# A decoder layer with experts on one core: expert rows fetched five tiles ahead, and a head's convolution products taken from cyclic copies that ScalarE writes

## The chip, the core and the metric

The kernel runs on one core of a Trainium2 chip. The metric is the device time of one execution in microseconds (us). Engines by their names in the profile: PE is TensorE (PEld its weight loads), DVE is VectorE, ACT is ScalarE, POOL is GpSimd, SP is SyncE; SP, ACT and POOL also start DMAs. On chip data lies in SBUF, 128 partitions wide, and PE writes to PSUM.

## What is computed

```python
x = x + attn(layernorm(x))                               # 16 heads, ALiBi, 16 x 256 tokens of 512
x = x + conv(k=ctx, v=ctx, q=layernorm(x), ssm_kernel, D)  # below
x = x + experts(layernorm(x))                            # top 2 of 8, silu-gated, 512 -> 256 -> 512

# conv: B=16, H=32 heads of 8 channels, length L=512
kv = einsum('bhil,bhjl->bijhl', k_, v_)                  # all 8 x 8 channel pairs of a head
y = irfft(rfft(kv, 2L) * rfft(ssm_kernel, 2L))[..., :L]  # causal convolution along L
out = einsum('bijhl,bhil->bjhl', y + kv * D, q_)
```

Since k and v are both the context, the pair (i, j) equals (j, i): 36 of the 64 pairs are distinct.

## The kernel before

The program has four stages, one after another: attention (up to about 720 us of the profiled execution), the convolution (743 to 1144), routing with the split of the expert weights (1156 to 1300), and the expert tiles (1300 to 1803).

**Convolution.** L lies across the partitions, in four chunks of 128 (EC). The batches are done in two groups g of 8 (GB), and in a group the 32 heads (SH) one after another: 64 steps in all, with h the head's number. Everything of a head has two buffers, by its parity. For one head and one group:
- POOL, `form_pairs` (L1037), multiplies the context by itself into `pairs`, 36 columns for each of 4 x 8 (chunk, batch): 8 TENSOR_TENSORs, one for each run of pairs that `pair_segments` gives, 1152 elements a partition. It waits for PE to be done with head h-2 (y_ready).
- PE, `convolve` (L1087), multiplies `pairs` by `taps` (a skewed view of the filter that SP loads): 10 products of 288 columns, which are 20 MATMUL records, into the PSUM tile `ps_y`. It waits for the pairs, the taps, and until DVE has read the `ps_y` of head h-2 (prods_ready).
- DVE, `multiply` (L1155), multiplies `ps_y` by q into `prods`, 15 TENSOR_TENSORs of 32 to 256 elements, 2048 in all. The eight terms of one sum lie side by side in `prods`, so each instruction writes its elements 8 apart (32 bytes).
- POOL, `fold` (L1046), adds the last two of the eight terms to the first two (512 elements).
- DVE, `add_up` (L1174), sums the remaining six (one TENSOR_REDUCE, 1536 elements) back over q.

DVE's order is multiply(h), add_up(h-1), multiply(h+1), add_up(h). POOL's is form_pairs(h), fold(h-2). ACT has nothing to do while the heads run.

**Experts.** The token rows are sorted by expert into 72 tiles of 128 (N_TILES). The loops are unrolled by RING tiles (8 before); rings of BUFS = 4 hold the fetched rows `srow` and the outputs `y_row`. For tile n:
- SP loads `pair_row` (which tokens), DVE `read_pairs` turns it into the indices `take` and `back`.
- POOL, `gather` (L1492), fetches 128 rows of 2 KB from DRAM into `srow` by an indirect DMA. POOL's step for tile n is: gather(n + AHEAD) with AHEAD = 3, wait for `y_row` of tile n, wait until the scatter of tile n-1 has landed, then the scatter of tile n, an indirect DMA that adds `y_row` to the output in DRAM (L1513). Tiles of one expert have no token in common, tiles of two experts may.
- PE's step for tile n is: transposes of the rows of tile n+2 (`s_transposes`, L1588), `h_transposes` of tile n (L1612), `gate_and_up` of tile n+1 (L1601, 12 matmuls), `down_rows` of tile n (L1621). So the rows of tile n+3 are needed at the start of step n+1.
- ACT and DVE move tiles from PSUM to SBUF between these steps; ACT's `weigh` (L1705) writes `y_row`.

## Time and profile before

| what | value |
|---|---|
| time, median of 3 runs | 1803.71 us (1803.37 to 1810.03) |
| the profiled execution | 1810.99 us, its span 1809.1 us |
| mean granted clock of PE | 0.929 of full |
| PE busy / DVE / ACT / POOL | 84% / 63% / 38% / 39% of the span |
| convolution, one head | 5.65 us, 64 heads |
| expert tiles | 72, from 1304 us to the end |

The span runs from the first to the last instruction; 1.9 us of the execution lie around it. Busy shares are averages over four stages that have different limits, so they are read by stage.

### The profile page before, as it was taken

The page shows a single profiled execution, that of the slowest core. Times are in us where ns is not written, and L with a number is a line of the kernel's source. Part 1 is how long each engine was busy: PE and PEld are TensorE (multiplying, and loading weights), DVE is VectorE, ACT ScalarE, POOL GpSimd, SP SyncE. Part 2 cuts the span into 40 slices and gives each one's busy share as a digit, 9 for nine tenths or more (in the row PEclk, how much of TensorE's full clock was granted, in tenths as well). Part 3 has the DMA queues.
Part 4 walks back from the last instruction along what each step waited for, and adds up shares of the span by engine and source line. Part 5 has one row for each costly group of instructions (what it writes and reads, how often), then busy time and mean ns, then how long its engine had stood idle before and what let it go on. Part 6 is the DMA issues. An engine that isn't in the chain of part 4 may idle for free. (4 is left out here: it accounts for less than half of the span.)

```text
span 1809.1 us, 34128 instructions
## 1 busy us (share of the span) xinstructions
PE 1513.5 (84%) x8665; PEld 1192.7 (66%) x8666; DVE 1141.0 (63%) x3591; ACT 678.5 (38%) x1818; POOL 712.3 (39%) x1160
## 2 busy tenths in 40 slices
PE   4999999999999997799968888667187888878886
PEld 4888888888888885666656666567155555555554
DVE  5788777777777776699989999866422222222221
ACT  3777677767676776100001000023122222222222
POOL 2111111111111101688846888266633343344343
PEclk9999999999999999999989999655599999899999
DMA  5543333433343445411131111369534444344441
GB/s 168 122 106 95 94 93 93 110 94 93 95 109 92 109 97 216 151 46 47 46 116 36 47 45 34 128 162 259 128 66 74 76 72 73 66 78 79 72 79 35
DMA packets 89767, 172.13 MB, mean 95 GB/s; under 512 B 26384, under 2 KB 26384, under 8 KB 88656
## 3 DMA queue, kind: packets, MB, share of 16 engines
q1 hardware_dynamic: 63584, 122.46, 25.3%
q0 software_dynamic: 18176, 35.80, 11.0%
q10 hardware_dynamic: 7920, 12.93, 2.8%
q8 instruction: 27, 0.44, 0.1%
q14 instruction: 60, 0.49, 0.1%
HBM read 78.10 MB, written 44.79 MB: 68 GB/s over the span
## 5 line engine op out<-in xcount | busy, mean ns | idle before, releaser
L1097 PE MATMUL ps_y<-pairs,taps 128*128 128x288 f32 x1280 | 324.5, 410 | 35.4 <-DVE prods L1170 32.1
L1097 PEld LDWEIGHTS ps_y<-pairs,taps 128*128 128x128 f32 x1280 | 238.3, 190 | 121.1 <-POOL pairs L1041 41.6
L853 ACT ACTIVATE probs<-neg_scores,neg_max 128x256 f32<-128x256 f32 x512 | 255.2, 505 | 26.1 <-DVE neg_max L654 25.9
L1170 DVE TENSOR_TENSOR prods<-ps_y,q_g 128x224 f32<-128x224 f32 (+7 forms) x960 | 251.3, 402 | 17.7 <-issue 8.0
L654 DVE CUSTOM_DVE_ANT_0 neg_scores<-ps_scores,alibi 128x256 f32<-128x256 f32 x512 | 194.8, 418 | 91.0 <-PE ps_scores L519 60.4
L1041 POOL TENSOR_TENSOR pairs<-ctx_g 128x32 f32 (+11 forms) x512 | 215.5, 460 | 43.0 <-PE ps_y L1097 31.8
L1513 POOL DMA_INDIRECT out<-y_row,back x72 | 113.2, 1573 | 293.1 <-ACT y_row L1705 158.3
L1894 DVE TENSOR_TENSOR st_lo<-ps_x,st_hi 128x512 fp32r<-128x512 f32 x72 | 49.8, 691 | 249.2 <-ACT st_hi L1690 249.2
L863 ACT ACTIVATE probs_t<-ps_probs_t 128x512 f32<-128x512 f32 x208 | 124.0, 596 | 130.5 <-PE ps_probs_t L530 130.4
L530 PE MATMUL ps_probs_t<-ident,probs 128*128 128x128 f32 x1024 | 159.2, 279 | 8.9 <-ACT probs L853 8.9
L1588 PE MATMUL ps_x<-ident,srow 128*128 128x128 f32 x288 | 49.1, 296 | 121.0 <-DMA srow<-xn_rows,take 120.8
L1588 PEld LDWEIGHTS ps_x<-ident,srow 128*128 128x128 f32 x288 | 32.5, 146 | 175.9 <-DMA srow<-xn_rows,take 95.8
L403 POOL COPY inv_wide<-inv_sum 128x512 f32<-128x512 f32 x32 | 20.6, 672 | 318.1 <-DVE inv_sum L670 318.1
L530 PEld LDWEIGHTS ps_probs_t<-ident,probs 128*128 128x128 f32 x1024 | 124.3, 143 | 22.7 <-ACT probs L853 9.4
L1621 PE MATMUL ps_down<-w_down,hidden_t 128*128 x288 | 135.3, 592 | 0.6 <-DVE hidden_t L1884 0.6
L519 PE MATMUL ps_scores<-k_stack,q_stack 96*128 96x256 f32 x512 | 128.5, 334 | 6.3 <-DMA k_stack<-k_lo 5.7
L1601 PE MATMUL ps_gu<-w_gu_hi,st_hi 128*128 x288 | 124.7, 433 | 0.3 <-DVE st_lo L1894 0.3
L1050 POOL TENSOR_TENSOR prods<-prods 128x512 f32<-128x512 f32 x64 | 98.6, 1541 | 64.9 <-DVE prods L1170 64.9
L1601 PE MATMUL ps_gu<-w_gu_hi,st_lo 128*128 x288 | 117.9, 409 | 0.0
L1601 PE MATMUL ps_gu<-w_gu_lo,st_hi 128*128 x288 | 117.6, 408 | 0.0
L1888 DVE TENSOR_TENSOR hidden<-ps_gu,silu_g 128x256 f32<-128x256 f32 x72 | 30.6, 424 | 131.4 <-ACT silu_g L1697 131.4
L1176 DVE TENSOR_REDUCE q_g<-prods 128x1536 f32 (+1 forms) x64 | 110.4, 1725 | 0.6 <-POOL prods L1050 0.6
(185 smaller groups left out, 3287.2 us busy)
## 6 DMA issues: line engine op xcount, KB each, us to landing
q_stack<-q_hi SPq DMA_DIRECT2D x128, 128.0 KB, 2.3
k_stack<-k_hi SPq DMA_DIRECT2D x128, 128.0 KB, 2.3
taps<-kernel_pad SPq DMA_DIRECT2D x64, 256.0 KB, 3.1
x_in<-in_x SPq DMA_DIRECT2D x16, 512.0 KB, 3.5
q_stack<-q_lo SPq DMA_DIRECT2D x64, 128.0 KB, 2.3
k_stack<-k_lo SPq DMA_DIRECT2D x64, 128.0 KB, 2.3
x_rows<-x_mid SPq DMA_DIRECT2D x16, 512.0 KB, 3.0
ctx_g<-in_ctx_t SPq DMA_DIRECT2D x2, 4096.0 KB, 12.4
```

The lines of the kernel that those rows point to most:

```text
L519: last = pe.matmul(ps_scores[h % 2][:, tt, :], q_stack[:, r, c, tt * P:tt * P + P], k_stack[:, r, c, :], start=True, stop=True)
L530: last = pe.transpose(ps_probs_t[h % 2][:, jt, tt * P:tt * P + P], probs[h % 2][:, tt, jt * P:jt * P + P], ident[:])
L654: last = dve.tensor_tensor_reduce(neg_scores[h % 2][:, tt, :], ps_scores[h % 2][:, tt, :], alibi[h % 2][:, P - P * tt:P - P * tt + T], -Q_ ...
L853: last = act.activation(probs[h % 2][:, tt, :], neg_scores[h % 2][:, tt, :], ACT.Exp, bias=neg_max[par][:, h, tt:tt + 1], scale=-1.0, accu ...
L863: act.activation(probs_t[h % (2 * HPC)][:], ps_probs_t[h % 2][:], ACT.Copy).then_inc(probs_t_kept[h % 2], 1)
L1041: last = pool.tensor_tensor(pairs[par][:, :, :, col:col + n], head_of(ctx_g, k * 2 + par, i, n), head_of(ctx_g, k * 2 + par, j, n), ALU.mult)
L1097: last = pe.matmul(ps_y[par][:, lc, 0:GB * PAIRS], taps[r][:, block_cols:block_cols + P], pairs[par][:, mc, :, :], start=(mc == 0), stop=( ...
L1170: last = dve.tensor_tensor(prods[par][:, :, :, to:to + n, term], y[:, :, :, col:col + n], head_of(q_g, own, q_from, n), ALU.mult)
L1176: dve.tensor_reduce(head_of(q_g, k * 2 + par, 0, SD), prods[par][:, :, :, :, 0:SD - FOLD], AX_X, ALU.add).then_inc(z_ready, 1)
L1513: pool.indirect_dma_start(out=out_rows, out_offset=bass.IndirectOffsetOnAxis(ap=back[r][:, 0:1], axis=0), in_=y_row[r % BUFS][:], in_offse ...
L1601: last = pe.matmul(ps_gu[:, r % 2, :], st[r % 2][x_part][:, c, :], w_gu[w_part][:, ds(e, 1), c, :].rearrange("p o f -> p (o f)"), start=(c ...
L1621: last = pe.matmul(ps_down[:, r % 2, :], hidden_t[r % 2][:, c, :], w_down[:, ds(e, 1), c, :].rearrange("p o f -> p (o f)"), start=(c == 0) ...
```

## The change

Two independent edits, one in the convolution and one in the expert stage.

**Convolution.** With d the cyclic distance of the two channels of a pair, `pairs` is now formed by two POOL instructions: all pairs with d = 0 to 3 at once (1024 elements), reading the context's 8 channels and a doubled copy of them, `ctx_ring`, at a moving start, and the four with d = 4 (128 elements). ACT writes `ctx_ring` (512 elements) and, for q, `q_ring` (512). When PE is done with a head, ACT copies `ps_y` into `y_rows`, with the first elements of each row repeated behind it: three ACTIVATEs of 1024, 288 and 256 elements. DVE then multiplies `y_rows` by `q_ring` in four instructions (one of 1280 elements, three of 256) that read and write consecutive elements, with the eight terms of a sum now 8 elements apart; one TENSOR_REDUCE of all 2048 reads them at that stride. `fold` is gone. PE waits for ACT's copy (y_kept) instead of DVE's products, DVE too.

**Experts.** RING 12, AHEAD 5, and six `srow` buffers (ROW_BUFS); `y_row` keeps four. The scatter of tile n waits for the landing of tile n-2, and for that of tile n-1 only where the expert changes. Which it is stands in a table, `tile_wait_i`, that DVE computes in three more instructions in routing, and POOL reads by a register load ahead of each scatter.

```diff
@@ convolution, POOL
-                    for col, i, j, n in pair_segments():
-                        last = pool.tensor_tensor(pairs[par][:, :, :, col:col + n],
-                                                  head_of(ctx_g, k * 2 + par, i, n),
-                                                  head_of(ctx_g, k * 2 + par, j, n), ALU.mult)
-                    last.then_inc(pairs_ready, 1)
-                def fold(g, k, par):
...
+                    wait_apart(pool, ctx_ring_ready, k * 2 + (g * SH + par + 1), passed)
+                    own = by_lane(ctx_g, k * 2 + par)
+                    to = pairs[par][:, :, :, :].rearrange("p m b q -> p (m b) q")
+                    pool.tensor_tensor(to[:, :, 0:HALF * SD].rearrange("p n (d i) -> p n d i", i=SD),
+                                       own.unsqueeze(2).to_broadcast([P, EC * GB, HALF, SD]),
+                                       turned(ctx_ring[par], HALF), ALU.mult)
+                    pool.tensor_tensor(to[:, :, HALF * SD:PAIRS], own[:, :, 0:HALF], own[:, :, HALF:SD], ALU.mult)\
+                        .then_inc(pairs_ready, 1)
@@ convolution, PE
-                    pe.wait_ge(prods_ready, h + (1 - 2 + PRODS_START))
+                    pe.wait_ge(y_kept, h + (1 - 2 + KEPT_START))
@@ convolution, ACT (head h: keep_y, then turn_ctx of head h + 2)
+                def turn_ctx(g, k, par):
...
+                        act.wait_ge(pairs_ready, k * 2 + (g * SH + par - 1))
...
+                    ring_of(ctx_ring[par], ctx_g, k * 2 + par).then_inc(ctx_ring_ready, 1)
+                def keep_y(g, k, par):
+                    act.wait_ge(prods_ready, h + (1 - 2 + PRODS_START))
+                    ring_of(q_ring[par], q_g, k * 2 + par)
+                    act.wait_ge(y_ready, h + (1 + Y_START))
...
+                    act.activation(whole_rows[:, :, :, 0:SD], near, ACT.Copy)
+                    act.activation(whole_rows[:, :, 0:HALF - 1, SD:ROW], near[:, :, 1:HALF, SD - HALF + 1:SD], ACT.Copy)
+                    act.activation(rows[:, :, HALF * ROW:ROWS].rearrange("p n (u i) -> p n u i", u=2),
...
+                                   ACT.Copy).then_inc(y_kept, 1)
@@ convolution, DVE
+                    dve.wait_ge(y_kept, h + (1 + KEPT_START))
                     dve.wait_ge(z_ready, h + (1 - 2 + Z_START))
...
+                    dve.tensor_tensor(prods[par][:, :, 0:HALF + 1, :], main_rows(y_rows[par], HALF + 1),
+                                      turned(q_ring[par], HALF + 1), ALU.mult)
+                    for e in range(HALF + 1, SD):
+                        d = SD - e
+                        last = dve.tensor_tensor(prods[par][:, :, e, :], y_rows[par][:, :, d * ROW - d:d * ROW - d + SD],
+                                                 q_ring[par][:, :, e:e + SD], ALU.mult)
...
+                    dve.tensor_reduce(by_lane(q_g, k * 2 + par), prods[par][:].rearrange("p n e i -> p n i e"), AX_X,
@@ experts, POOL
-        RING = 8
+        RING = 12
-        AHEAD = 3
+        ROW_BUFS = 6
+        AHEAD = 5
...
+                        landed = pool.value_load(tile_wait_i[0:1, ds(tile_no(kk, r) - 1, 1)], min_val=16,
+                                                 max_val=N_TILES // BUFS * 16)
                     wait_apart(pool, y_ready, tile_no(kk, r) + 1 + Y_START, passed)
-                        wait_apart(pool, y_scattered[(r - 1) % BUFS], turn(kk, r - 1) * 16 + 16, passed)
+                        wait_apart(pool, y_scattered[(r - 2) % BUFS], turn(kk, r - 2) * 16 + 16, passed)
...
+                        wait_apart(pool, y_scattered[(r - 1) % BUFS], landed, passed)
@@ routing, DVE
+                chain(dve.tensor_tensor(new_expert[:, 0:N_TILES - 1], tile_expert[:, 1:N_TILES],
+                                        tile_expert[:, 0:N_TILES - 1], ALU.not_equal))
+                dve.scalar_tensor_tensor(tile_wait_i[:, 0:N_TILES - 1], new_expert[:, 0:N_TILES - 1], 16.0,
+                                         turn_f[:, 0:N_TILES - 1], ALU.mult, ALU.add).then_inc(tiles_known, 1)
```

DVE's queue in the loop over heads, before, for one head (the sum between is that of the head before):

```order
L1170 TENSOR_TENSOR prods<-ps_y,q_g 128x256
L1170 ISA
L1170 TENSOR_TENSOR prods<-ps_y,q_g 128x32x7 x2
L1170 TENSOR_TENSOR prods<-ps_y,q_g 128x32
L1170 ISA
L1170 TENSOR_TENSOR prods<-ps_y,q_g 128x32
L1170 ISA
L1170 TENSOR_TENSOR prods<-ps_y,q_g 128x32x6 x2
```

The same place of DVE's queue now, the four products of one head and the sum of the head before:

```order
L1208 TENSOR_TENSOR prods<-y_rows,q_ring 128x32x40
L1212 TENSOR_TENSOR prods<-y_rows,q_ring 128x32x8 x3
L26 ISA
L1220 ISA
L1220 TENSOR_REDUCE q_g<-prods 128x32x8
```

Fifteen products that read PSUM and q have become four that read two SBUF tiles. ACT's queue at the same place, empty before, now holds for one head:

```order
L1135 ACTIVATE q_ring<-q_g 128x512
L1151 REGISTER_ALU
L1156 ACTIVATE y_rows<-ps_y 128x32x4x8
L1157 ACTIVATE y_rows<-ps_y 128x32x3x3
L1158 ACTIVATE y_rows<-ps_y 128x32x8
L1141 ISA
L1135 ISA
L1135 ACTIVATE ctx_ring<-ctx_g 128x512
```

The copy of the context for head h+2 stands behind the three copies of head h. POOL's queue at the start of the expert tiles, before:

```order
L1500 DMA srow<-xn_rows,take 128x512 x4
L1513 DMA out<-y_row,back 4096x512
L1500 DMA srow<-xn_rows,take 128x512
L1513 DMA out<-y_row,back 4096x512
L1500 DMA srow<-xn_rows,take 128x512
```

And now, from the start:

```order
L1555 DMA srow<-xn_rows,take 128x512 x6
L1577 DMA out<-y_row,back 4096x512
L1555 DMA srow<-xn_rows,take 128x512
L1577 DMA out<-y_row,back 4096x512
L1555 DMA srow<-xn_rows,take 128x512
```

Six fetches stand ahead of the first scatter instead of four. From the sixth tile on it reads:

```order
L1555 DMA srow<-xn_rows,take 128x512
L1565 TENSOR_LOAD tile_wait_i
L1565 ISA x2
L1577 DMA out<-y_row,back 4096x512
L1555 DMA srow<-xn_rows,take 128x512
```

A register load now stands between the fetch and the scatter.

## Rows read from the trace of the kernel before

**Rows 1.** Stretches: us; PE, PEld, DVE, ACT, POOL busy; clock; DMA share; GB/s
```profile
780.00:900.00 120.00, 108.18 (x427) 79.08 (x427) 116.89 (x337) 0.00 (x0) 102.98 (x191) 1.00 0.17 47
...
1324.00:1540.00 216.00, 173.86 (x702) 116.99 (x703) 49.83 (x160) 52.37 (x95) 83.08 (x64) 0.98 0.42 74
```
**Rows 2.** PE in order of time, heads: start, us, op, [idle before <-releaser]
```profile
808.03 5.09 PE L1097 MATMUL ps_y<-pairs,taps 128*128 128x288 f32 x20 [0.56 <-DVE prods L1170]
```
**Rows 3.** DVE in order of time, the same heads
```profile
803.95 3.93 DVE L1170 TENSOR_TENSOR prods<-ps_y,q_g 128x256 f32<-128x256 f32 x15
807.74 1.73 DVE L1176 TENSOR_REDUCE q_g<-prods 128x1536 f32 x1
```
**Rows 4.** Who waited for whom, 1300 to 1800 us: total, times, longest
```profile
PE ps_x L1588 <- DMA srow<-xn_rows,take: 120.8, 60, 26.1
```
**Rows 5.** The transposes of the fetched rows, L1588: ns min/median/max, first and last start
```profile
L1588 PE MATMUL ps_x<-ident,srow x288: 272/273/475, 1304.3 to 1787.9; 128*128 128x128 f32 x144
```
**Rows 6.** The chain that ended last, 1400 to 1440 us
```profile
1412.63 0.70 ACT y_row L1705
...
1414.32 0.02 POOL out L1513
...
1416.20 4.32 DMA srow<-xn_rows,take
```
**Rows 7.** PE in order of time around one tile whose rows had landed
```profile
1550.41 1.88 PE L1621 MATMUL ps_down<-w_down,hidden_t 128*128 x4
1552.13 0.60 PE L1588 MATMUL ps_x<-ident,srow 128*128 128x128 f32 x4
...
1555.55 1.88 PE L1621 MATMUL ps_down<-w_down,hidden_t 128*128 x4
1559.44 0.66 PE L1588 MATMUL ps_x<-ident,srow 128*128 128x128 f32 x4 [2.02 <-DMA srow<-xn_rows,take]
```
**Rows 8.** POOL in order of time, expert tiles
```profile
1537.95 1.58 POOL L1513 DMA_INDIRECT out<-y_row,back  x1 [6.20 <-issue]
1539.84 1.05 POOL L1500 DMA_INDIRECT srow<-xn_rows,take  x1 [0.30 <-issue]
1543.70 1.57 POOL L1513 DMA_INDIRECT out<-y_row,back  x1 [2.81 <-DMA out<-y_row,back]
```
**Rows 9.** Register loads of SP, L1442 (columns as in rows 5)
```profile
L1442 SPq TENSOR_LOAD <-tile_row_i x72: 263/268/480, 1296.7 to 1750.8; - x72
```
**Rows 10.** DVE, groups by form: busy, mean ns, idle before
```profile
L1170 DVE TENSOR_TENSOR prods<-ps_y,q_g 128x256 f32<-128x256 f32 x64 | 40.1, 626 | 17.7 <-issue 8.0 <-DVE q_g L1176 2.4 <-PE ps_y L1097 0.8
...
L1888 DVE TENSOR_TENSOR hidden<-ps_gu,silu_g 128x256 f32<-128x256 f32 x72 | 30.6, 424 | 131.4 <-ACT silu_g L1697 131.4
...
L1402 DVE TENSOR_TENSOR w_gu_lo<-w_half,w_gu_hi 128x1024 f32 x4 | 4.9, 1226 | 2.3 <-DVEq L1809 2.3
```
**Rows 11.** ACT, groups by form
```profile
L863 ACT ACTIVATE probs_t<-ps_probs_t 128x512 f32<-128x512 f32 x208 | 124.0, 596 | 130.5 <-PE ps_probs_t L530 130.4
...
L1132 ACT ACTIVATE q_g<-ps_y 128x1024 f32 x16 | 16.3, 1027 | 223.1 <-PE ps_y L1083 223.1
```
**Rows 12.** POOL, groups by form
```profile
L1402 POOL TENSOR_TENSOR w_gu_lo<-w_half,w_gu_hi 128x1024 fp32r<-128x1024 f32 x4 | 9.4, 2354 | 0.7 <-ACT w_gu_hi L1658 0.7
...
L1041 POOL TENSOR_TENSOR pairs<-ctx_g 128x128 f32 x60 | 27.4, 456 | 0.0
```
**Rows 13.** DVE in order of time, routing
```profile
1225.87 1.23 DVE L1402 TENSOR_TENSOR w_gu_lo<-w_half,w_gu_hi 128x1024 f32 x1 [0.55 <-DVEq L1809]
...
1256.85 0.19 DVE L1757 TENSOR_TENSOR is_best<-ps_gu,best 128x32 f32<-128x32 f32 x1
1257.18 0.63 DVE L1758 TENSOR_TENSOR is_best<-is_best,backward 128x32 f32<-128x32 f32 x1
```
**Rows 14.** POOL in order of time, routing
```profile
1226.45 2.85 POOL L1402 TENSOR_TENSOR w_gu_lo<-w_half,w_gu_hi 128x1024 f32 x1 [4.19 <-ACT w_gu_hi L1658]
...
1254.94 2.82 POOL L1402 TENSOR_TENSOR w_gu_lo<-w_half,w_gu_hi 128x1024 f32 x1 [1.15 <-ACT w_gu_hi L1658]
```

More of the change, by code:

```diff
@@ L961, in build_decoder @@
         TAP_BUFS = 4
-        FOLD = 2
-        def pair_segments():
-            segments = [(0, 0, 0, SD)]
-            for d in range(1, SD // 2):
-                segments += [(d * SD, 0, d, SD - d), (d * SD + SD - d, SD - d, 0, d)]
-            return segments + [(SD // 2 * SD, 0, SD // 2, SD // 2)]
+        HALF = SD // 2
+        ROW = SD + HALF - 1
+        ROWS = HALF * ROW + SD
         with ExitStack() as scope:
@@ L981, in build_decoder @@
             pairs = [sb(f"pairs{i}", [P, EC, GB, PAIRS]) for i in range(2)]
-            prods = [sb(f"prods{i}", [P, EC, GB, SD, SD]) for i in range(2)]
+            prods = [sb(f"prods{i}", [P, EC * GB, SD, SD]) for i in range(2)]
+            y_rows = [sb(f"y_rows{i}", [P, EC * GB, ROWS]) for i in range(2)]
+            q_ring = [sb(f"q_ring{i}", [P, EC * GB, 2 * SD]) for i in range(2)]
+            ctx_ring = [sb(f"ctx_ring{i}", [P, EC * GB, 2 * SD]) for i in range(2)]
             xn_g = [sb(f"xn_g{i}", [P, TT, E]) for i in range(2)]
@@ L1062, in _ @@
                             form_pairs(g, k, par)
-                            fold(g, k - 1, par)
-                    for par in range(2):
-                        fold(g, SH // 2 - 1, par)
                 pool.wait_ge(x2_moments, GT)
@@ L1096, in convolve @@
                             block_cols = (lc - mc) * P
-                            last = pe.matmul(ps_y[par][:, lc, 0:GB * PAIRS], taps[r][:, block_cols:block_cols + P],
+                            last = pe.matmul(ps_y[par][:, lc, :].rearrange("p (b q) -> p b q", b=GB)[:, :, 0:PAIRS],
+                                             taps[r][:, block_cols:block_cols + P],
                                              pairs[par][:, mc, :, :], start=(mc == 0), stop=(mc == lc))
@@ L1123, in _, with ring_of @@
                 act.sem_inc(c_xt_kept, XT_START)
+                act.sem_inc(y_kept, KEPT_START)
+                def ring_of(to, tile, h):
+                    return act.activation(to[:].rearrange("p n (u i) -> p n u i", u=2),
+                                          by_lane(tile, h).unsqueeze(2).to_broadcast([P, EC * GB, 2, SD]), ACT.Copy)
+                def turn_ctx(g, k, par):
+                    if not (isinstance(k, int) and k == 0):
+                        act.wait_ge(pairs_ready, k * 2 + (g * SH + par - 1))
+                    elif g:
+                        act.wait_ge(pairs_ready, SH)
+                    ring_of(ctx_ring[par], ctx_g, k * 2 + par).then_inc(ctx_ring_ready, 1)
+                def keep_y(g, k, par):
+                    h = k * 2 + (par + g * SH)
+                    act.wait_ge(prods_ready, h + (1 - 2 + PRODS_START))
+                    ring_of(q_ring[par], q_g, k * 2 + par)
+                    act.wait_ge(y_ready, h + (1 + Y_START))
+                    y = ps_y[par][:].rearrange("p c (b q) -> p (c b) q", b=GB)
+                    near = y[:, :, 0:HALF * SD].rearrange("p n (d i) -> p n d i", i=SD)
+                    rows = y_rows[par]
+                    whole_rows = rows[:, :, 0:HALF * ROW].rearrange("p n (d r) -> p n d r", r=ROW)
+                    act.activation(whole_rows[:, :, :, 0:SD], near, ACT.Copy)
+                    act.activation(whole_rows[:, :, 0:HALF - 1, SD:ROW], near[:, :, 1:HALF, SD - HALF + 1:SD], ACT.Copy)
+                    act.activation(rows[:, :, HALF * ROW:ROWS].rearrange("p n (u i) -> p n u i", u=2),
+                                   y[:, :, HALF * SD:PAIRS].unsqueeze(2).to_broadcast([P, EC * GB, 2, HALF]),
+                                   ACT.Copy).then_inc(y_kept, 1)
                 for g in range(2):
+                    act.wait_ge(ctx_load, 16 * g + 16)
+                    for par in range(2):
+                        turn_ctx(g, 0, par)
                     with act.Fori(0, GB // 2) as k:
@@ L1135, in _ @@
                         act.dma_start(x_res[:, GT:NT, :], x1_tiles[:, GT:NT, :]).then_inc(x1_load[1], 16)
+                    act.wait_ge(c_xt_kept, (g + 1) * GB + XT_START)
+                    with act.Fori(0, SH // 2 - 1) as k:
+                        for par in range(2):
+                            keep_y(g, k, par)
+                            turn_ctx(g, k + 1, par)
+                    for par in range(2):
+                        keep_y(g, SH // 2 - 1, par)
             @block.vector
@@ L1284, in build_decoder @@
                 back = [sb_in(tiling, f"back{i}", [P, 1], U32) for i in range(RING)]
-                srow = [sb_in(tiling, f"srow{i}", [P, E]) for i in range(BUFS)]
+                srow = [sb_in(tiling, f"srow{i}", [P, E]) for i in range(ROW_BUFS)]
                 st = [[sb_in(tiling, f"st_{part}{i}", [P, EC, P], F32R) for part in ("hi", "lo")] for i in range(2)]
@@ L1330, in build_decoder @@
             take_ready = sem("take_ready")
-            row_load = [sem(f"row_load{i}") for i in range(BUFS)]
+            row_load = [sem(f"row_load{i}") for i in range(ROW_BUFS)]
             st_done = sem("st_done")
```

77 lines of the change are left out of this document (42 added, 35 removed).

## The prediction

> **What bounds the kernel now.** I read the stretches first, one in each stage that the change touches [rows 1], and then each stage in order of time.
>
> In the convolution PE shows 90% busy at full clock and DVE 97% [rows 1]. The order of time says which one decides: PE's 20 matmuls of a head take 5.09 us, and before them PE stands 0.56 us until DVE's products are done [rows 2], while DVE goes without a gap through products (3.93) and sum (1.73) [rows 3]. A head is 5.09 + 0.56 = 5.65 us. So DVE sets 64 heads of 5.65 us, 362 us, and PE could go at 5.1.
>
> In the expert tiles no engine is near full: PE 80%, DVE 23% [rows 1]. What PE waits for is the fetched rows: 120.8 us in 60 waits, of which 26.1 is the wait for the first tile after routing [rows 4]. 94.7 us lie inside the loop. 71 tiles from the first transposes to the last take 483.6 us [rows 5], 6.8 each. The chain shows the loop that makes the waits: `y_row` written, the scatter's issue 1.0 us behind it, only then on POOL the next fetch, 3.6 us after `y_row` began, and 4.32 us to its landing [rows 6]; then PE's transposes and the rest up to the `y_row` of that tile. With a fetch three tiles ahead this loop spans two tiles, 2 x 6.8 = 13.6 us. PE's own step is shorter. Where rows had landed, the transposes start 1.72 us after `down_rows` (1550.41 to 1552.13), and `down_rows` 3.42 us after them (to 1555.55): 5.14 us [rows 7].
>
> **The expert edit.** The fetch for tile n+6 now follows the scatter of tile n, and PE needs it at step n+4: the same loop spans four tiles, 13.6 / 4 = 3.4 us a tile, under PE's 5.14. The waits in the loop go: 94.7 us [rows 4]. Each of the 59 is counted only from the modelled end of the last matmul (1.88 us), 0.16 after the 1.72 at which a next op starts [rows 7]: 9.4 us more. Against it, the granted clock is 0.98 here [rows 1]; part of its half-speed pieces fell into waits and will fall on work: I give back 2. Sum: **-102 us**. The other way: 71 steps of 5.14 are 365 us, 119 less than 483.6, and the half-speed clock in the first tiles and at the later dips, some 15 us of which I leave in, comes off.
>
> What is late next? POOL: its two issues take 1.57 and 1.05 with 0.30 between them [rows 8], and 1.0 us lies between `y_row` and the start of the scatter (1413.33 to 1414.32) [rows 6]; with a register load of 0.27 to 0.5 (SP's) [rows 9] that is 4.2 to 4.4 us, under 5.14, and the load stands ahead of the wait for `y_row`, beside the DMA issue. The old wait for the scatter before allowed no less than 5.75 us a tile (1537.95 to 1543.70, ended by a landing) [rows 8]: it is gone but for the 7 changes of expert, where the lead of the fetches covers it. If it stayed, the price is rival 3. The three more instructions in routing cost below 1 us, and the DMAs to the row table end later than they do: nothing. SP's longer ring costs nothing, its loads are asked for by tiles twelve back. Bounds for the edit: -115 (nothing given back) to -85 (waits go, a few come back at the expert changes and behind late landings).
>
> **The convolution edit.** DVE per head: two rows give a slope for consecutive elements, (1226 - 424) / 768 = 1.04 ns, and 0.16 us fixed [rows 10]. The product of 1280: 1.49 us; three of 256: 0.35 each where they overlap, 1.05; together 2.55. The old products wrote at a stride, and their 256 took 626 ns, not 424 [rows 10]: that is what the four new ones save. The sum: 2048 elements at 1.04 plus 0.12 are 2.25 if reading at a stride of 32 bytes is free. No row has DVE reading fp32 at a stride; the nearest row is the strided write, (626 - 160) / 256 = 1.8 ns, which would make it 3.85. I take 2.25, since the only row at the higher price is a write and every sum in the trace, this one's 1536 elements in 1.73 us too [rows 3], goes at the slope for consecutive ones; 3.85 stays as rival 2. DVE then needs 4.8 us a head, below PE.
>
> But the products now have two inputs in SBUF, and POOL reads SBUF too. The trace shows what that does: POOL's 1024-element TENSOR_TENSOR takes 2.35 us alone [rows 12]; begun at 1226.45 while DVE worked on a product of two SBUF tiles until 1227.1, it took 2.85 [rows 14]. And DVE's small product of two SBUF tiles at 1257.18 took 0.63 us and ended when POOL's did (1254.94 + 2.82 = 1257.76), while one with a PSUM input just before it, beside the same POOL instruction, took 0.19 [rows 13, 14]. So each holds the other off for a whole instruction; today's products read PSUM and one SBUF tile and are not held.
>
> The Trainium skill has this as a rule (SBUF — State Buffer, "Who interferes with whom"): a DVE instruction with two SBUF inputs and a GpSimd one that reads SBUF share a read port under an exclusive lock, and the second waits for the whole first. It speaks against this edit, and by this trace it holds. Without it the loop below would have ACT's copy (0.60) where DVE's product stands (1.49), 5.3 us a head, 30 us less in all.
>
> The loop from head h to h+2 (both of one parity) is then: ACT's copies of 1024, 288 and 256 elements, 1.03 + 0.41 + 0.38 = 1.82 (1027 and 596 ns for 1024 and 512, slope 0.84) [rows 11]; now ACT's copy of the context (0.60) and DVE's product of 1280 (1.49) start together, and POOL, which waits for the copy, finds DVE at it: 1.49; POOL's two products, 2.35 + 0.46 = 2.81 [rows 12]; PE 5.09 [rows 2]; five hand-overs of 0.05. That is 11.46 us for two heads, **5.73 a head**, against 5.65: +5 us for 64 heads, and with ACT's copies now ahead of the first products of both groups (2 x 1.8) about +8. POOL itself is relieved: 2.8 us a head instead of 4.9. Bounds: POOL finds the port free and the loop falls below PE's own work, 5.09 less a little overlap from head to head: 5.05, -38 us. POOL waits for all four products: 12.5 us for two, 6.25 a head, +38 us.
>
> **Sum.** 1811.0 (profiled execution, its span and 1.9 us around it) - 102 + 8 = 1717; the median of the runs is 7.3 us below the profiled one, and the same sum there gives 1803.7 - 94 = **1710 us**.
>
> **Rivals.**
> 1. *The port closes a loop over every head, slower than before.* ACT copies q of head h only when the products of h-2 are done, and copies `ps_y` behind that. If DVE falls one head behind, so that POOL always meets it at a first product, the loop is: product 1.49, POOL 2.81 (DVE's other three wait), 1.05, ACT's q copy 0.60 and copies 1.82, hand-overs 0.25: 8.0 us for one head, +152 us: 1803.7 - 102 + 152 = 1854. It decides when a head takes over 5.65 + 102/64 = 7.24 us. For it: products and pairs together hold the port 2.55 + 2.81 = 5.36 us of each head, nearly all of it, and with two buffers a lost lead is not easily made up. Against it: DVE has to lose its lead first. Chance 0.17.
> 2. *The sum reads at the price of the strided write*: 3.85 instead of 2.25, DVE 6.4 us a head and the bound, +49 us: 1803.7 - 102 + 52 = 1754. For it: the 626 ns row. Against: that row is a write. Chance 0.15. The Trainium skill speaks for it (SBUF — State Buffer, "Door 1: The DMA port swizzle"): full rate wants at least two accesses in one 16-byte line. The trace's write agrees, no row shows a read.
> 3. *The tiles don't reach PE's step*: landing waits or POOL's queue keep 5.75 us, +0.6 x 71 = +43: 1710 + 43 = 1753. For it: the old spacing in rows 8. Against: POOL's sum of 4.5. Chance 0.10.
> 4. *The convolution gains as meant*, port conflicts falling into DVE's sum: 5.05 to 5.2 a head, 1803.7 - 102 - 35 = 1667. Chance 0.15.
> My forecast, 1690 to 1735, has 0.38; mixtures make the last 0.05.
>
> **How the numbers follow.** Faster by over 0.5% (about what a measurement of this kernel can tell from no change) means below 1794.7: all but rival 1 and the mixtures that come near it, 0.79. Within 0.5%: 0.04. Slower: 0.17. The range has to leave out no more than 2 in 10: rival 1 at its full price stays out (0.17), mixtures of it with rival 2 come in: 1658 to 1815.
>
> **What would show it.** Right: in the tiles PE's waits for `srow` below 20 us in all and a step near 5.2; in the convolution PE's idle time ended by `pairs`, no longer by `prods`, POOL's 1024-element products at 2.4 us or longer with DVE's 1280-element one ending as they begin. Wrong: the sum at over 3 us (rival 2), DVE's 256-element products at 2 to 3 us and ACT's q copy waiting for `prods` (rival 1), POOL's larger product below 2 us (rival 4), scatters spaced 5.7 us by a landing (rival 3). The forecast is most wrong if the heads lock into the loop of rival 1.

## The result, and the profile after

The changed kernel takes 1843.3 us (median, 1841.5 to 1844.7) against 1805.2 us before: 1.021 times as long, with an interval of 1.018 to 1.023. The prediction was 1710 us, 1658 to 1815. So the kernel became slower where it was forecast faster, and the time lies outside the range.

The profiled span went from 1809.1 to 1843.0 us. By stage, from the starts of PE's and DVE's first and last instructions in both traces:

| stretch | before | after | difference |
|---|---|---|---|
| start to the first matmul of the heads | 743.1 | 749.0 | +5.9 |
| first to last matmul of the heads | 391.5 | 521.9 | +130.4 |
| from there to the start of routing | 22.0 | 33.1 | +11.1 |
| routing, to the first transposes of fetched rows | 147.8 | 152.4 | +4.6 |
| expert tiles | 504.8 | 386.6 | -118.2 |

The expert edit did what it was expected to do. The convolution edit cost more than that. The same two stretches as in [rows 1], one inside each stage, in the kernel after (us; PE, PEld, DVE, ACT, POOL busy; clock; DMA share; GB/s):

```profile
780.00:900.00 120.00, 88.73 (x316) 63.45 (x314) 119.49 (x75) 41.92 (x78) 60.41 (x32) 0.93 0.13 36
1473.00:1689.00 216.00, 216.00 (x919) 150.99 (x918) 65.20 (x207) 65.60 (x126) 108.66 (x83) 1.00 0.57 99
```

In the tiles PE never stops in this stretch. Who waited for whom there, and the transposes of the fetched rows (ns min/median/max, first and last start), which answer to [rows 4, 5]:

```profile
POOL out L1577 <- DMA out<-y_row,back: 140.6, 62, 3.6
...
PE ps_x L1653 <- DMA srow<-xn_rows,take: 25.8, 2, 25.6
```
```profile
L1653 PE MATMUL ps_x<-ident,srow x288: 270/273/476, 1456.4 to 1822.1; 128*128 128x128 f32 x144
```

Of PE's waits for rows the first tile's is left, 25.6 us, and one of 0.2 us. A tile takes (1822.1 - 1456.4) / 71 = 5.15 us, against 6.8. POOL still waits for landings, 62 times, and nobody waits for POOL.

In the heads DVE is busy in 119.49 of 120 us, but the profile counts an engine as busy also while its instruction is held, that is, begun and waiting for the other engine to let go of the read port. The groups of the convolution, from the page (busy, mean ns, idle before and its releaser), for [rows 2, 3, 12]:

```profile
L1103 PE MATMUL ps_y<-pairs,taps 128*128 128x288 f32 x1280 | 357.8, 440 | 121.6 <-POOL pairs L1058 116.5
...
L1055 POOL TENSOR_TENSOR pairs<-ctx_g,ctx_ring 128x1024 f32<-128x1024 f32 x64 | 149.6, 2338 | 296.5 <-ACT ctx_ring L1135 296.5
L1220 DVE TENSOR_REDUCE q_g<-prods 128x2048 f32 (+1 forms) x64 | 247.5, 3870 | 0.0
...
L1208 DVE TENSOR_TENSOR prods<-y_rows,q_ring 128x1280 f32<-128x1280 f32 x64 | 167.6, 2619 | 13.5 <-issue 11.4
```

PE's idle time is ended by `pairs`, as forecast. But the sum takes 3.87 us, not 2.25, and the product of 1280 takes 2.62 on average, not 1.49. In order of time it is the same pattern from the sixth head of a group on (start, us, engine, line, [idle before <-releaser]):

```profile
853.42 3.89 DVE L1220 TENSOR_REDUCE q_g<-prods 128x2048 f32 x1
...
861.43 3.88 DVE L1220 TENSOR_REDUCE q_g<-prods 128x2048 f32 x1
861.63 0.63 ACT L1135 ACTIVATE q_ring<-q_g 128x512 f32 x1 [5.28 <-DVE prods L1212]
862.17 1.08 ACT L1156 ACTIVATE y_rows<-ps_y 128x1024 f32<-128x1024 f32 x1
863.13 0.47 ACT L1157 ACTIVATE y_rows<-ps_y 128x288 f32<-128x288 f32 x1
863.46 0.38 ACT L1158 ACTIVATE y_rows<-ps_y 128x256 f32<-128x256 f32 x1
863.71 0.64 ACT L1135 ACTIVATE ctx_ring<-ctx_g 128x512 f32 x1
864.62 2.29 POOL L1055 TENSOR_TENSOR pairs<-ctx_g,ctx_ring 128x1024 f32<-128x1024 f32 x1 [4.06 <-ACT ctx_ring L1135]
865.34 2.91 DVE L1208 TENSOR_TENSOR prods<-y_rows,q_ring 128x1280 f32<-128x1280 f32 x1
866.86 1.70 POOL L1058 TENSOR_TENSOR pairs<-ctx_g 128x128 f32 x1
```

DVE's sum begins at 861.43, right behind the last small product. The same end of the products releases ACT, which copies q, `ps_y` and the context in a row, and that releases POOL 3.19 us after the sum's start. The sum lasts 3.88. So POOL is 0.7 us into its reading when DVE comes to the next product, and the product, 1.49 us of work, waits until POOL is done at 866.91, 1.57 us, and ends at 868.25. POOL's second instruction, 0.46 us of work, takes 1.70 behind it. One head earlier the sum began at 853.42: the loop takes 861.43 - 853.42 = 8.01 us.

### The profile page after: what moved, and what is told of

The parts are those of the page before. It is cut to its first block and busy times, and to the rows that moved or that the text cites. A ratio compares the mean times of both kernels' runs of the same rounds, so it can differ in the third digit from the quotient of the medians.

```text
span 1843.0 us, 33019 instructions
## 1 busy us (share of the span) xinstructions
PE 1526.1 (83%) x8665; PEld 1208.8 (66%) x8666; DVE 1287.8 (70%) x2890; ACT 847.0 (46%) x2138; POOL 645.1 (35%) x714
## 5 line engine op out<-in xcount | busy, mean ns | idle before, releaser
L1103 PE MATMUL ps_y<-pairs,taps 128*128 128x288 f32 x1280 | 357.8, 440 | 121.6 <-POOL pairs L1058 116.5
L1103 PEld LDWEIGHTS ps_y<-pairs,taps 128*128 128x128 f32 x1280 | 258.1, 205 | 220.8 <-POOL pairs L1058 105.6
L1055 POOL TENSOR_TENSOR pairs<-ctx_g,ctx_ring 128x1024 f32<-128x1024 f32 x64 | 149.6, 2338 | 296.5 <-ACT ctx_ring L1135 296.5
L1220 DVE TENSOR_REDUCE q_g<-prods 128x2048 f32 (+1 forms) x64 | 247.5, 3870 | 0.0
L1208 DVE TENSOR_TENSOR prods<-y_rows,q_ring 128x1280 f32<-128x1280 f32 x64 | 167.6, 2619 | 13.5 <-issue 11.4
L1577 POOL DMA_INDIRECT out<-y_row,back x72 | 113.2, 1572 | 174.8 <-DMA out<-y_row,back 140.6
L1135 ACT ACTIVATE q_ring<-q_g 128x512 f32 (+1 forms) x64 | 40.4, 631 | 271.1 <-DVE prods L1212 270.5
L1666 PE MATMUL ps_gu<-w_gu_hi,st_hi 128*128 x288 | 121.0, 420 | 0.2 <-DVE st_lo L1964 0.2
L643 DVE TENSOR_SCALAR alibi<-dist_neg,slope_scaled 128x384 f32<-128x384 f32 x256 | 110.8, 433 | 0.0
L1762 ACT ACTIVATE silu_g<-ps_gu 128x256 f32<-128x256 f32 x72 | 27.6, 384 | 165.3 <-PE ps_gu L1666 165.3
```

Source lines behind the costliest of these rows:

```text
L1055: pool.tensor_tensor(to[:, :, 0:HALF * SD].rearrange("p n (d i) -> p n d i", i=SD), own.unsqueeze(2).to_broadcast([P, EC * GB, HALF, SD]), ...
L1103: last = pe.matmul(ps_y[par][:, lc, :].rearrange("p (b q) -> p b q", b=GB)[:, :, 0:PAIRS], taps[r][:, block_cols:block_cols + P], pairs[pa ...
L1208: dve.tensor_tensor(prods[par][:, :, 0:HALF + 1, :], main_rows(y_rows[par], HALF + 1), turned(q_ring[par], HALF + 1), ALU.mult)
L1220: dve.tensor_reduce(by_lane(q_g, k * 2 + par), prods[par][:].rearrange("p n e i -> p n i e"), AX_X, ALU.add).then_inc(z_ready, 1)
L1577: pool.indirect_dma_start(out=out_rows, out_offset=bass.IndirectOffsetOnAxis(ap=back[r][:, 0:1], axis=0), in_=y_row[r % BUFS][:], in_offse ...
L1666: last = pe.matmul(ps_gu[:, r % 2, :], st[r % 2][x_part][:, c, :], w_gu[w_part][:, ds(e, 1), c, :].rearrange("p o f -> p (o f)"), start=(c ...
```

## The experiments

Times are medians of four executions for the kernel after, e1 and e6; the others are single executions with their profile. The runs are from several chips, on which the kernel before took between 1801.9 and 1809.3 us, so a difference of a few us between two runs says little. "Heads" is the time from PE's first to its last matmul of the 64 heads: 391.5 us before, 521.9 after.

### The two edits apart

`e1_tiles_only` is the kernel before with the expert edit and its three routing instructions, `e2_conv_only` the kernel before with the convolution edit.

```diff
@@ e1_tiles_only, against the kernel before
-        RING = 8
+        RING = 12
-        AHEAD = 3
+        ROW_BUFS = 6
+        AHEAD = 5
...
+                        wait_apart(pool, y_scattered[(r - 1) % BUFS], landed, passed)
@@ e2_conv_only, against the changed kernel
-        RING = 12
+        RING = 8
-        AHEAD = 5
+        AHEAD = 3
```

> The kernel before with the expert edit alone. If the two edits add up: the expert stage takes what it takes in the changed kernel, 386.6 us from the first transposes to the end of the span instead of 504.8, so 1804 - 118 = 1686 us (1680 to 1692). If the faster tiles were a gift of the slower convolution (another clock, another alignment), it ends at 1700 or more, with granted clock below 1.0 in the tiles.

> The kernel before with the convolution edit alone. If the edits add up: +147 us for the convolution and +5 ahead of the tiles, 1955 us (1945 to 1965), 8.0 us a head. If part of the loss came from the expert edit, below 1940.

Measured: e1 1695.2 us, 0.938 times the kernel before (0.934 to 0.941); e2 1941.6 us. The first line is e1's tiles (the stretch of [rows 1]), the second e2's heads:

```profile
1324.00:1540.00 216.00, 216.00 (x919) 150.98 (x918) 64.92 (x207) 65.59 (x126) 109.36 (x84) 1.00 0.56 99
```
```profile
800.00:900.00 100.00, 70.84 (x248) 50.98 (x249) 99.58 (x65) 34.40 (x63) 48.52 (x25) 0.92 0.12 34
```

The expert edit alone makes the kernel 6% faster, and the stage takes 386.2 us in e1 and 386.6 with both edits. The convolution edit is the whole loss: 521.8 us of heads in e2. e1 came out 9 us above what was expected, and e2 13 below, both outside their ranges. On e1's chip the kernel before took 1809.3 us, so the gain there is 114 us where 118 was expected. The 13 us of e2 lie in the part of the program that is the same as before: its tiles took 490.9 us, not 504.8, at a mean granted clock of 0.99, where the kernel before has 0.96 (its line stands further below):

```profile
1449.00:1910.00 461.00, 371.06 (x1516) 247.03 (x1516) 108.50 (x343) 115.59 (x208) 176.85 (x135) 0.99 0.43 76
```

### The sum and the port, one by one

Two suspects: the stride at which the sum reads, and POOL's reading beside DVE's products. `e3_sum_consecutive` and `e4_pool_reads_nothing` take one away each, `e5_neither` both. None of the three computes the layer: e3 and e5 add up other products than they should, e4 and e5 form no pairs.

```diff
@@ e3, e5: DVE
-                    dve.tensor_reduce(by_lane(q_g, k * 2 + par), prods[par][:].rearrange("p n e i -> p n i e"), AX_X,
+                    dve.tensor_reduce(by_lane(q_g, k * 2 + par), prods[par][:], AX_X,
@@ e4, e5: POOL
-                    pool.tensor_tensor(to[:, :, 0:HALF * SD].rearrange("p n (d i) -> p n d i", i=SD),
...
-                    pool.tensor_tensor(to[:, :, HALF * SD:PAIRS], own[:, :, 0:HALF], own[:, :, HALF:SD], ALU.mult)\
+                    pool.memset(to[:, :, 0:HALF * SD], 0.5)
+                    pool.memset(to[:, :, HALF * SD:PAIRS], 0.5).then_inc(pairs_ready, 1)
```

> The changed kernel, but the sum of a head reads the 2048 products as they lie (consecutive), so that it adds other elements together; nothing else differs. The sum should take 2.26 us instead of 3.87. Theory A, the loop through the port (ACT's copies, POOL's pairs, DVE's products in turn, which the sum is not part of) holds a head at 8.0 us whatever the sum takes: 1835 to 1843 us. Theory B, the long sum made DVE late and only with it the loop closed: DVE gets its lead back, 5.1 to 5.8 us a head, about 1665 to 1710 us.

> The changed kernel, but POOL fills the pairs with a constant by two memsets (1024 and 128 elements, about 1.3 us in all instead of 2.7) and reads no SBUF; the pairs of the context are left out. If the held port makes the loop: DVE's product of 1280 takes 1.49 us in every head instead of 2.6 to 2.9, a head takes DVE's own 1.49 + 1.05 + 3.87 = 6.4 us, and the whole is 1843 - 64 x 1.6 = 1740 us. If the strided sum alone set the 8.0 us, or a memset holds DVE off as well, the product stays above 2 us and the time above 1800.

> The changed kernel with both suspected costs taken away: POOL fills `pairs` with a constant and reads nothing (so it cannot hold DVE's two-SBUF-input products), and DVE's sum reads `prods` as they lie. The context pairs are left out and the sum adds other elements together, so the time is that of the same instruction counts with less work in two places. If the two costs add up one after the other (each worth its own on DVE): DVE needs 1.49 + 1.05 + 2.27 = 4.8 us a head, under PE's 5.1, so PE sets the head: 64 x 5.1 + the start, 1843 - 64 x 2.9 = 1655 to 1670. If there is a third cost in the convolution that neither explains (ACT's copies, hand-overs): the head stays above 5.3 us and the time above 1680.

| | POOL reads | POOL reads nothing |
|---|---|---|
| sum at a stride | 1843.3 us, heads 521.9 | e4: 1749.5, heads 423.5 |
| sum consecutive | e3: 1714.6, heads 408.1 | e5: 1651.4, heads 344.9 |

e3 and e4 ended 5 and 10 us above what the theory of a held port and a dear stride gave, e5 4 below. Over e5, the stride alone costs 98 us, the port alone 63, both together 192: 31 more than their sum. In the heads alone it is 79, 63 and 177, 35 more than the sum. Most of the stride's other 20 us lie behind the last matmul, where DVE still has its sums to do: from there to the start of routing e4 takes 35.8 us and e5 21.4. e3 in order of time, two heads:

```profile
838.85 2.29 POOL L1055 TENSOR_TENSOR pairs<-ctx_g,ctx_ring 128x1024 f32<-128x1024 f32 x1 [4.03 <-ACT ctx_ring L1135]
839.40 3.10 DVE L1208 TENSOR_TENSOR prods<-y_rows,q_ring 128x1280 f32<-128x1280 f32 x1
...
843.68 2.27 DVE L1220 TENSOR_REDUCE q_g<-prods 128x2048 f32 x1
843.70 2.31 POOL L1055 TENSOR_TENSOR pairs<-ctx_g,ctx_ring 128x1024 f32<-128x1024 f32 x1 [0.89 <-ACT ctx_ring L1135]
...
845.99 1.78 DVE L1208 TENSOR_TENSOR prods<-y_rows,q_ring 128x1280 f32<-128x1280 f32 x1
...
851.00 3.28 DVE L1208 TENSOR_TENSOR prods<-y_rows,q_ring 128x1280 f32<-128x1280 f32 x1
```

The sum now takes 2.27 us, so that DVE mostly reaches its next product earlier. Only every second head is held for long, and two heads take 851.00 - 839.40 = 11.6 us: 5.8 a head against the 5.73 of the prediction's loop over two heads. The order is not the prediction's, though. There POOL came second and waited for the product in every head. Here POOL's larger instruction comes first, in every second head: the product waits (3.10 for 1.49), and only POOL's small instruction waits behind it. In the other heads the product takes 1.78. In e4 nothing is held:

```profile
853.28 1.49 DVE L1205 TENSOR_TENSOR prods<-y_rows,q_ring 128x1280 f32<-128x1280 f32 x1
...
855.70 3.87 DVE L1217 TENSOR_REDUCE q_g<-prods 128x2048 f32 x1
...
858.78 0.95 POOL L1055 MEMSET pairs<- 128x1024 f32 x1 [5.22 <-ACT ctx_ring L1132]
859.61 1.49 DVE L1205 TENSOR_TENSOR prods<-y_rows,q_ring 128x1280 f32<-128x1280 f32 x1
```

The sum is still 3.87 us with POOL reading nothing: the stride is its price, not POOL. The product is 1.49 us although POOL is at work when it starts. A head is 6.33 (853.28 to 859.61), DVE's own work: 1.49 + 1.0 + 3.87, less a little overlap. In e5 DVE has time to spare and PE never stops:

```profile
800.00:900.00 100.00, 99.67 (x411) 77.74 (x410) 96.91 (x105) 54.71 (x102) 21.96 (x40) 1.00 0.22 67
```

### Where POOL's reading falls

e4 also made POOL's work shorter. To keep POOL's work whole and only move it, ACT's copy of the context, which starts POOL, changes its place in ACT's queue.

```diff
@@ e7_ring_first, ACT
+                            turn_ctx(g, k + 1, par)
                             keep_y(g, k, par)
-                            turn_ctx(g, k + 1, par)
@@ e9_ring_at_sum_start, ACT, in keep_y
                     act.wait_ge(prods_ready, h + (1 - 2 + PRODS_START))
+                    if more:
+                        turn_ctx(g, k + 1, par)
                     ring_of(q_ring[par], q_g, k * 2 + par)
...
-                            keep_y(g, k, par)
-                            turn_ctx(g, k + 1, par)
+                            keep_y(g, k, par, True)
```

> The changed kernel with two lines of ACT's queue exchanged: the copy of the context for head h+2 (`ctx_ring`) stands ahead of head h's copies of q and of `ps_y`, not behind them. Nothing else is changed, nothing left out. In the changed kernel POOL begins its pairs 0.7 us before DVE's sum is over, since it waits for that copy, and so meets the next head's products. With the copy early, POOL waits for PE's last matmul alone, about 2.5 us earlier, and its 2.75 us lie under DVE's 3.87-us sum, which has one SBUF input. Theory (the place where POOL falls, not its reading as such, is what costs 1.6 us a head): L1208 near 1.5 us, head 6.35 to 6.5, DVE's own 2.5 + 3.87: 1750 to 1765, as with a POOL that reads nothing. Rival (any POOL read in the loop costs DVE the same, wherever it falls): head near 8.0, 1835 to 1845.

> The changed kernel with ACT's copy of the context for head h+2 put between ACT's wait for the products of head h-2 and its copies of q and `ps_y`, all in keep_y of head h. All is computed, nothing else changed. The run with that copy merely ahead of keep_y left POOL where it was (it began 3.2 us after DVE's products ended, 0.7 us before the sum's end), because ACT's queue stands in the wait for those products either way. Here the copy is the first thing ACT does when the products end, so POOL should begin about 0.85 us after them and be through 3.6 us after them, inside the 3.87-us sum. Theory (what costs 1.6 us a head is that POOL's read falls on a product and not on the sum): L1208 near 1.5 us, L1058 near 0.46, head 6.35 to 6.6, 1750 to 1770. Rival (POOL's read costs DVE the same wherever it falls, or is shifted to another product): L1208 or L1212 stay long, head near 8, 1835 to 1850.

e7 measured 1841.0 us, and my expectation for it was wrong. The order of its instructions differs, their phase doesn't:

```profile
860.23 3.86 DVE L1220 TENSOR_REDUCE q_g<-prods 128x2048 f32 x1
860.43 0.63 ACT L1135 ACTIVATE q_ring<-q_g 128x512 f32 x1 [5.29 <-DVE prods L1212]
...
863.41 2.30 POOL L1055 TENSOR_TENSOR pairs<-ctx_g,ctx_ring 128x1024 f32<-128x1024 f32 x1 [4.06 <-ACT ctx_ring L1135]
864.12 2.94 DVE L1208 TENSOR_TENSOR prods<-y_rows,q_ring 128x1280 f32<-128x1280 f32 x1
```

ACT stands in the wait for DVE's products, whatever is queued behind it. The copy ran right behind the `ps_y` copies of the head before, so POOL began 3.18 us after the sum's start again. e9 puts the copy directly behind that wait: 1759.7 us, heads 435.0.

```profile
857.75 3.88 DVE L1221 TENSOR_REDUCE q_g<-prods 128x2048 f32 x1
857.98 0.63 ACT L1135 ACTIVATE ctx_ring<-ctx_g 128x512 f32 x1 [3.55 <-DVE prods L1213]
...
858.87 2.31 POOL L1055 TENSOR_TENSOR pairs<-ctx_g,ctx_ring 128x1024 f32<-128x1024 f32 x1 [3.56 <-ACT ctx_ring L1135]
...
861.13 0.46 POOL L1058 TENSOR_TENSOR pairs<-ctx_g 128x128 f32 x1
...
861.67 1.49 DVE L1209 TENSOR_TENSOR prods<-y_rows,q_ring 128x1280 f32<-128x1280 f32 x1
```

POOL begins 1.12 us into the sum and is done at 861.59, the sum at 861.63. All of the reading is there, the port is the same, and neither is held. One copy in another place of a queue is worth 84 us. What costs is where POOL's reading falls. The heads of e9 still take 11.5 us more than those of e4, most of it in the first four of a group, where the first two products take 2.19 and 2.23 us.

The Trainium skill says this of the chip (SBUF — State Buffer, "Who interferes with whom"): a DVE instruction with two SBUF inputs contends with a GpSimd instruction that reads SBUF, and a reduction never contends on trn2. This trace agrees: 3.88 us for the sum beside POOL, 3.87 without.

### The stride at the other end

`e8_write_strided` is the changed kernel with the stride moved from the sum's read to the products' writes.

```diff
-                    dve.tensor_tensor(prods[par][:, :, 0:HALF + 1, :], main_rows(y_rows[par], HALF + 1),
+                    dve.tensor_tensor(prods[par][:, :, :, 0:HALF + 1].rearrange("p n i e -> p n e i"), main_rows(y_rows[par], HALF + 1),
...
-                        last = dve.tensor_tensor(prods[par][:, :, e, :], y_rows[par][:, :, d * ROW - d:d * ROW - d + SD],
+                        last = dve.tensor_tensor(prods[par][:, :, :, e], y_rows[par][:, :, d * ROW - d:d * ROW - d + SD],
...
-                    dve.tensor_reduce(by_lane(q_g, k * 2 + par), prods[par][:].rearrange("p n e i -> p n i e"), AX_X,
+                    dve.tensor_reduce(by_lane(q_g, k * 2 + par), prods[par][:], AX_X,
```

> The changed kernel with the stride moved from the sum's read to the products' writes: the four products write their elements 8 apart, as the kernel before does, and the sum reads consecutive ones (2.27 us). All is computed. Theory (a 32-byte stride costs DVE 1.8 ns an element on either side): the product of 1280 takes 2.3 to 2.5 us when POOL does not hold it, a product of 256 about 0.63, products and sum together 6.4 us as before the move, and the head stays at 7.2 to 8.2 us, 1790 to 1855. Rival (the price is one of reading alone, or of the reduce alone, and the strided write of the kernel before was slow for its PSUM input): products 2.55, sum 2.27, 1714 as with the consecutive sum.

Measured: 1846.2 us, heads 537.2.

```profile
855.07 2.25 DVE L1220 TENSOR_REDUCE q_g<-prods 128x2048 f32 x1
...
857.35 2.49 DVE L1208 TENSOR_TENSOR prods<-y_rows,q_ring 128x1280 f32<-128x1280 f32 x1
857.43 0.64 ACT L1135 ACTIVATE ctx_ring<-ctx_g 128x512 f32 x1
858.33 3.51 POOL L1055 TENSOR_TENSOR pairs<-ctx_g,ctx_ring 128x1024 f32<-128x1024 f32 x1 [4.05 <-ACT ctx_ring L1135]
...
859.68 3.77 DVE L1212 TENSOR_TENSOR prods<-y_rows,q_ring 128x256 f32<-128x256 f32 x3
...
863.30 2.25 DVE L1220 TENSOR_REDUCE q_g<-prods 128x2048 f32 x1
```

The write at a stride costs (2.49 - 0.16) / 1280 = 1.82 ns an element, the read in the changed kernel (3.87 - 0.12) / 2048 = 1.83. The price is the same on both sides, so that a transposition between two SBUF tiles can't be had free by choosing the side. POOL begins 3.26 us after the sum does (855.07 to 858.33), about as in the changed kernel, but a sum of 2.25 us is over by then. So here it is DVE that comes first: POOL is held 1.2 us beyond its 2.3, then DVE's small products wait for POOL, 3.77 us in place of some 1.9 (an estimate, three times the 626 ns of [rows 10]). A head is 8.23 us (855.07 to 863.30). So either order costs, and what helps is that the two don't meet.

### A convolution without either cost

`e6_psum_strided` keeps the expert edit and POOL's two instructions for the pairs. It drops `y_rows`: DVE multiplies `ps_y` in PSUM directly, which leaves one SBUF input, and does the transposition in the PSUM read. The sum reads consecutive elements, and POOL folds two of eight terms as before.

```diff
@@ against e1_tiles_only, DVE
-                    for col, i, j, n in pair_segments():
...
+                    for i, e, ni, ne, start, step in PARTS:
+                        last = dve.tensor_tensor(prods[par][:, :, i:i + ni, e:e + ne],
+                                                 y_part(ps_y[par], start, ni, ne, step),
+                                                 q_part(q_ring[par], i, e, ni, ne), ALU.mult)
@@ the parts: channel, term, their counts, start and step in PSUM
+        PARTS = [(0, 0, 4, 5, 0, 8), (4, 0, 4, 4, 4, 8), (4, 4, 4, 4, 32, -7),
+                 (0, 5, 3, 1, 29, -7), (0, 6, 2, 1, 22, -7), (0, 7, 1, 1, 15, -7),
+                 (3, 5, 1, 3, 24, -7), (2, 6, 1, 2, 16, -7), (1, 7, 1, 1, 8, -7)]
```

> The expert edit with another convolution, which computes the whole layer: POOL forms the pairs in two instructions from `ctx_ring` as in the changed kernel, ACT writes only the two rings (no `y_rows`), and DVE multiplies `ps_y` in PSUM by `q_ring` directly, in nine instructions that walk PSUM at a stride of 32 bytes (28 backwards for the pairs of larger distance) and write runs of three to five consecutive elements; the eight terms lie side by side again, so the sum reads consecutive elements, POOL folds two of eight as before. No product has two SBUF inputs, so nothing is held by the port lock. If the price of a stride is one of SBUF and PSUM reads are free of it: products about 2048 x 1.04 ns plus the small ones at a stride, 2.3 to 2.8 us, sum 1.73, DVE 4.0 to 4.5 us a head, PE sets 5.1: 1695 - 64 x 0.5 = 1655 to 1670. If a strided PSUM read costs what the strided SBUF read does (1.8 ns an element): products 3.7 to 4.0, a head 5.5 to 5.8 as in the kernel with the expert edit alone, 1690 to 1705.

Measured: 1648.8 us (1646.7 to 1653.8), 0.916 times the kernel before (0.913 to 0.918), and heads 344.7. That is 6 us below the range expected, and faster than both kernels and than e1. A stretch, the products by form, and one head in order of time:

```profile
800.00:900.00 100.00, 100.00 (x414) 78.34 (x413) 92.96 (x210) 23.05 (x40) 87.81 (x62) 1.00 0.19 50
```
```profile
L1220 DVE TENSOR_TENSOR prods<-ps_y,q_ring 128x512 f32<-128x512 f32 x128 | 81.9, 681 | 0.0
L1220 DVE TENSOR_TENSOR prods<-ps_y,q_ring 128x640 f32<-128x640 f32 x64 | 52.9, 827 | 33.1 <-PE ps_y L1125 33.1
```
```profile
853.42 2.85 DVE L1220 TENSOR_TENSOR prods<-ps_y,q_ring 128x640 f32<-128x640 f32 x9 [0.35 <-PE ps_y L1125]
...
853.72 2.30 POOL L1068 TENSOR_TENSOR pairs<-ctx_g,ctx_ring 128x1024 f32<-128x1024 f32 x1 [0.57 <-PE ps_y L1125]
...
856.17 1.75 DVE L1227 TENSOR_REDUCE q_g<-prods 128x1536 f32 x1
...
858.27 2.85 DVE L1220 TENSOR_TENSOR prods<-ps_y,q_ring 128x640 f32<-128x640 f32 x9 [0.35 <-PE ps_y L1125]
```

POOL reads SBUF while DVE multiplies, and nobody is held (the product has one SBUF input). 640 elements read from PSUM 32 bytes apart take 0.83 us, (0.83 - 0.16) / 640 = 1.04 ns each, the price of consecutive ones. The bound is PE, at 858.27 - 853.42 = 4.85 us a head.

## Why the prediction was wrong, point by point

**The step that failed is the price of the sum.** The prediction took 2.25 us and kept 3.85 as rival 2, with 0.15; the sum takes 3.87. Every sum in the trace that had gone at 1.04 ns an element read consecutive elements, so none spoke of a stride. The one row that did, the 626-ns product, was set aside because it was a write. That row was the nearest, and it was right to 0.02 us: 1.8 ns an element where the prediction took 1.04, which took DVE from below PE's 5.1 us a head to 6.4, above it. The rule of the Trainium skill that the prediction put beside rival 2 (SBUF — State Buffer, "Door 1: The DMA port swizzle") was right too; the runs now show the read that the trace before lacked.

**The second failure: rivals 1 and 2 were priced as exclusive, and one starts the other.** Rival 2 alone is 1754 us, and e9 (1759.7) and e4 (1749.5) show its head of 6.4 us (6.33). That the totals agree as well is luck: the tiles gave 16 us more than was said and the heads took 8 to 20 less than the 52, while the stretches around the heads took 23 to 25 more, over half of it behind the last matmul. Rival 1 alone needed DVE to lose its lead, and the argument against it was that this has to happen first; at the 4.8 us a head of the prediction it would not. With the long sum DVE needs 6.4, has no lead, and from the sixth head of a group on meets POOL in every head: 8.01 us, which is rival 1's 8.0, and 1843 us where it said 1854.

The equal figure is in part luck too, for the loop isn't quite the one that rival 1 describes. From one end of the products to the next it is ACT's four copies, 3.19 us with the hand-overs, POOL's larger product 2.29, the rest of the product of 1280 1.34 and the small ones 1.19. The copy of the context (0.64) was not in rival 1's sum, and POOL's small product, which was, lies mostly beside DVE's. The sum itself isn't in this loop; its length decides who comes first. POOL starts 3.19 us after the sum does, and a sum of 3.88 lets POOL in first. With a sum of 2.25 that is over before POOL's start at 3.26, DVE comes first (e8), and with one of 2.27 POOL gets well ahead only in every second head (e3). Had the two been joined, the 0.15 of rival 2 would have counted nearly whole as slower.

**With the price of the sum as taken, the rest of the sum held.** e3 has a sum of 2.27 us and takes 1714.6 us, where the prediction said 1710, with the bound that it named: not DVE's work but the port between POOL and the product of 1280, 5.8 us a head against 5.73, if in another order than it thought. The total is closer than its parts: the heads took 16.6 us more than before and the stretch ahead of them 5.1, where 8 were said in all, and the tiles gave 16 us more than was said. The pieces were as priced: product of 1280 1.49 (when not held), three of 256 1.0 after it, POOL 2.29 + 0.46, ACT's three copies 1.7 from first start to last end (1.82).

**Rival 4's head is that of e5 and e6**, with PE as the bound: 1651 and 1649 us where it said 1667. No run has it with the edit's full work in these instructions, since e5 leaves work out. PE's floor is 4.85 us a head, not 5.05 to 5.2: the 5.09 us of [rows 2] contain a modelled end that in a full queue lies under the next head's first matmul.

**The expert edit: right mechanism, somewhat too small.** -102 us was said, the stage gave -118. The waits in the loop went as said. The 1.0 us from `y_row` to the scatter, POOL's old spacing of 5.75 us (rival 3) and the changes of expert all stayed off the path, since POOL's waits for landings, 140.6 us, hold up nobody. The mis-sized term is the clock. The prediction had 94.7 + 9.4 = 104 us for the waits, left some 15 us of half-speed pieces in and gave back 2 more. This is the tile stage before and after, in the columns of [rows 1]:

```profile
1304.00:1788.00 484.00, 387.95 (x1543) 261.21 (x1544) 109.83 (x346) 117.00 (x211) 181.32 (x139) 0.96 0.42 74
```
```profile
1456.00:1822.00 366.00, 364.70 (x1540) 255.40 (x1541) 110.09 (x346) 110.06 (x211) 179.84 (x138) 0.99 0.55 97
```

The mean granted clock rose from 0.96 to 0.99: nearly all pieces at the lower level of 1.2 GHz went. e2, with the tiles unchanged, shows the same clock at 13.9 us less than before. Taken off the -118, that leaves -104 for the waits, which is the prediction's term. So the clock term is what was mis-sized: -14 where the sum had +2. But e2 has this clock with 117.7 us of waits for rows still in it, so fuller tiles aren't needed for it; how much of the 13.9 us differs from execution to execution by itself, one run doesn't tell, and the cause of the better clock stays open. The sum's other way, 71 steps of 5.14, gave -119.

**Routing** was priced below 1 us and went up by 4.6. e1 has the same three instructions and takes 147.4 us, 0.4 less than before, and this stretch is between 146.3 and 155.3 us in the runs here. So it isn't the new instructions; what moves it is open. **From the last matmul to routing** 11 us were added that the prediction didn't name: PE's last matmul starts at 1270.9 and DVE's last two sums start only at 1284.18, with 7.5 us of work.

## What to carry to other kernels

Price an access by its layout: where the trace has no row for a strided read, the strided write of the same engine is the row to take, and a tile that is transposed between two instructions pays on one side or the other, unless the read comes from PSUM. When two engines share something exclusively, ask at which moment in the loop each comes to it and what fixes that moment: here a start 3.19 us into the sum in place of 1.12 cost 84 us, and the cure was one copy's place in a queue. And before rivals get chances of their own, ask whether one sets off another: both together cost 31 us more than the sum of the two.

## What the runs showed of the hardware

- DVE in fp32 takes 1.83 ns an element when it reads SBUF at 32 bytes' distance and 1.82 when it writes so, against 1.04 for consecutive elements, or for PSUM read at 32 bytes' distance.
- DVE's TENSOR_REDUCE, with one SBUF input, runs beside a reading POOL at no loss (3.88 and 3.87 us); a product of two SBUF tiles waits for all of POOL's instruction (1.49 becomes 2.9), and POOL's small one waits for it in turn (0.46 becomes 1.7). POOL filling a tile without reading holds up nobody (the product stays at 1.49 beside it in e4 and e5).
- An engine that is held is shown as busy: DVE's 99.6% of the heads contain 1.4 us of standing still in every 8.0 (2.91 for a product of 1.49), and some 0.25 more in the small products (1.34 for 1.09). The duration of one instruction against its shortest says it, the share doesn't.
- PE's mean granted clock was 1.00 in a stretch of the tiles in which PE never idled, and 0.93 in the heads of the changed kernel, where PE waits for pairs. Idle time alone doesn't set it: the tiles of e2 have 0.99 with 117.7 us of waits, those of the kernel before 0.96 with 120.8.
